# Indirect DMAs in place of a one-hot product for the int4 weight's permutation, and another step order ahead of the first FFN

## The chip, the cores and the metric

One core of a Trainium2 chip runs the whole program in one launch. The metric is the time on the device in microseconds (us), the median of several runs. TensorE is called PE below, VectorE DVE, ScalarE ACT, GpSimd POOL, SyncE SP.

## What is computed

Two gated layers over 8 batches of 128 tokens with 512 features. Each layer is cross attention (32 query heads, 8 key/value heads, head size 128, keys and values from a context of 128 tokens), then a feed-forward part:

```python
x = x + tanh(g_xattn[0]) * xattn(layernorm(x), ctx, mask, ...)      # layer 0
x = x + tanh(g_ffn[0]) * mx_ffn(layernorm(x), w_gate, w_up, w_down) # fp6 x fp4 block quantised, 1376 inner
x = x + tanh(g_xattn[1]) * xattn(layernorm(x), ctx, mask, ...)      # layer 1
x = x + tanh(g_ffn[1]) * int4_linear(layernorm(x))                  # this change
# int4_linear: y = x[:, perm] @ w.T + bias, w (512 x 512) from int4 pairs and a scale per 128 inputs
```

The columns of x are permuted by `perm`. The kernel permutes the weight instead: row `i` of the transposed weight has to stand at row `perm[i]`.

## The kernel before

**Units and steps.** A unit is one key/value group (with its 4 query heads) of one batch: 64 units a layer, 128 in all. The program runs in steps, one unit a step, software-pipelined: in step n PE makes K, V and Q of unit n (`three_products`, L1210), the scores of unit n-1 (L1274), the transposes of the probabilities of unit n-2 (L1202) and, at the end of the step, their product with V (`values`, L1301), and the output projection of unit n-3 (L1210, from oT). In between stand the transposes of the scaled K (L1291) and Q (L1202, from qn). Every fp32 product is three products of split operands (`_hi` and `_lo`, 4 k-tiles each).

**Kinds of steps.** 0 to 7 are FIRST. 8 to 47 are QUANT: beside attention they quantise one piece each of the first FFN's weight. 48 to 87 are ZONE, written out one by one: 48 to 55 still quantise pieces but run in the plain order, 56 (`FFN0`) to 74 hold the FFN's tiles (norm at 56, gate at 57, down at 58, and so on, a new tile every second step), and from 75 (`INT4_0`) on the int4 weight is made. 88 to 119 are PLAIN, the rest LAST, where the last linear layer runs with the permuted weight `wp_hi`, `wp_lo`. All engines run the same list of steps, each with its own code in the order written in its `step`.

**Order within a step.** In a QUANT step PE does the scores ahead of the probabilities' transposes, ACT does the exponentials of the unit before at the step's start (`exp_after`) and kT, DVE does qn ahead of the row maximum, and POOL subtracts the split weight (`split_lower`, L494) behind the rounding of the piece (`round_piece`, L532 to L537). In the other steps the probabilities come first, kT is DVE's (L1070), and POOL's splits stand at the step's start, ahead of `unit_rstd` (L519, L523). `unit_rstd` waits for ACT's sums of squares (L694); K's and Q's scaling, and so PE's transposes L1291 and L1202, wait for it.

**Weights.** SP loads each group's weight (`load_group`: wq, wk, wv once `kv_ps` and `q_ps` say that the slot is free, wo once `y_ps` does). ACT rounds 10 pieces of 512 columns to `w_hi` (L661), POOL subtracts (L494). Pieces 0 to 3 are Q's, 4 and 5 K's and V's, 6 to 9 wo's. `SPLIT_ZONE` says at which ZONE step each is done.

**The int4 weight before.** `int4_weights` (DVE, 8 parts in steps 75 to 82): two one-hot matrices from an iota of POOL's and `perm` (L955), nibbles (L961, L962), scaling (L969), and the split into `w4_hi` and `w4_lo` (L975, L979). In each of the steps 83 to 86 PE multiplies them with the one-hots in 8 matmuls of 512 columns (L1407). ACT copies `wp_hi` (L762), DVE `wp_lo` (L1104).

Of the kernel before, what the change touches and what calls it, by code (L numbers as in the profile page):

```python
# [14 lines left out]
P = 128  # L15
# [82 lines left out]
SPLIT_ZONE = {1: ((B, 0), (B, 1)), 2: ((B, 2), (B, 3)), 3: ((B, 4), (B, 5)), 4: ((B, 6), (B, 7)), 5: ((B, 8), (B, 9)),  # L98
# [34 lines left out]
INT4_PARTS = 8  # L133
# [19 lines left out]
def flamingo_kernel(nc, x, ctxT, mask, g_xattn, g_ffn, norms, wq, wk, wv, wo, ffn_w,  # L153
                    packedT, scalesT, perm, bias, out):
    top = ExitStack()
    with top:
# [3 lines left out]
        def sem(name):  # L160
# [22 lines left out]
        w4_hi = sb("w4_hi", [P, 2, 2, D], FP32R, under)  # L183
        w4_lo = sb("w4_lo", [P, 2, 2, D], FP32R, under)
# [58 lines left out]
        perm_f = sb("perm_f", [P, 2, 2])  # L243
# [41 lines left out]
        loaded_w4, loaded_bias, iota_done, nibbles, w4_scaled, w4_done, wp_ps, wp_hid, wp_lod, biased = (sem(n) for n in (  # L285
            "loaded_w4", "loaded_bias", "iota_done", "nibbles", "w4_scaled", "w4_done", "wp_ps", "wp_hid", "wp_lod", "biased"))
# [60 lines left out]
        def gathered(n, kind):  # L347


            at = n - INT4_0 - INT4_PARTS  # L350
            return (at,) if kind == ZONE and 0 <= at < KT else ()
# [5 lines left out]
        def qn_first(kind, t):  # L357

            return kind in (FIRST, QUANT) or t.down is not None or t.next is not None

        def exp_after(kind):

            return kind == QUANT
# [19 lines left out]
        def _(sp):  # L383
# [75 lines left out]
            sp.dma_start(perm_sb[:, :, :], perm.rearrange("(t p c) -> p t c", t=2, c=2)).then_inc(loaded_w4, 16)  # L459
            load_group(E, 0, None, step_of(C, BATCHES - 1) + 1)  # L460
            load_group(E + 1, 1)
            sp.wait_ge(wp_ps, KT)
            sp.dma_start(bias_sb[:, :], bias.partition_broadcast(P)).then_inc(loaded_bias, 16)
# [14 lines left out]
        def _(pool):  # L478
# [74 lines left out]
            def step(n, b, kind, j, q=None):  # L553
# [13 lines left out]
                if kind in (ZONE, PLAIN):  # L567
                    split_lower(split_pieces(n, b, kind, j))
# [943 lines left out]
```

## Time and profile before

| | us |
|---|---|
| median of 3 runs | 1347.76 |
| lowest and highest of them | 1346.44, 3458.26 |
| the profiled execution, whole | 1346.49 |
| its span in the profile | 1344.6 |
| PE busy | 1336.9 (99%) |
| DVE, ACT, POOL busy | 960.4, 837.0, 635.2 |

1.9 us of the profiled execution lie outside its span. The granted TensorE clock is full in all 40 slices. The sum of the prediction is made against 1346.49, which is 1.3 below the median and within 0.1 of the lowest run. PE's busy time comes from modelled ends of pipelined matmuls, so where PE stands is better read from the distance between starts of the same row in successive steps.

### The profile page before, as it was taken

To read this page: it belongs to the slowest core of one execution; us is meant where nothing else is said; L and a number is where in the kernel's file an instruction comes from. 1 tells how busy PE (TensorE), PEld (TensorE's weight loads), DVE (VectorE), ACT (ScalarE), POOL (GpSimd) and SP (SyncE) were. 2 spreads that over 40 slices of the span, in tenths; PEclk is the share of its full clock that TensorE was granted. 3 is DMA by queue.
4 is the path that set the end of the run, shared out by engine and by line. 5 is a ranking of instruction groups with operands and counts; after the bars stand their busy time and mean duration, and the time that the engine had idled before them with its cause. 6 is when DMAs were issued, how large, how long until landed. Compare 5 with 4: busy or idle time off the path is not lost.

```text
span 1344.6 us, 25713 instructions
## 1 busy us (share of the span) xinstructions
PE 1336.9 (99%) x7841; PEld 1135.6 (84%) x7841; DVE 960.4 (71%) x1984; ACT 837.0 (62%) x3299; POOL 635.2 (47%) x682
## 2 busy tenths in 40 slices
PE   9999999999999999999999999999999999999999
PEld 7888888888888888777777788888888888888887
DVE  6878787887878798788888857766555555555656
ACT  6767676676767675556656556655666656565542
POOL 3456556564646575356767424432434333332232
PEclk9999999999999999999999999999999999999999
DMA  8011212102121210010100022001010100100001
GB/s 291 1 60 50 67 50 65 52 22 64 49 66 49 67 50 21 1 48 32 49 32 1 1 79 79 32 1 56 32 47 31 45 33 0 47 31 1 2 8 56
DMA packets 32957, 59.49 MB, mean 44 GB/s; under 512 B 2928, under 2 KB 24304, under 8 KB 28784
## 3 DMA queue, kind: packets, MB, share of 16 engines
q1 hardware_dynamic: 32592, 58.01, 13.0%
q8 instruction: 39, 0.64, 0.2%
q10 hardware_dynamic: 288, 0.52, 0.1%
q14 instruction: 38, 0.31, 0.1%
HBM read 56.43 MB, written 2.10 MB: 44 GB/s over the span
## 4 chain that ended last, share of the span: by engine, by line
PE 96%; DVE 1%; POOL 1%; issue 1%; DMA 0%; ACT 0%; SPq 0%; POOLq 0%; DVEq 0%; ACTq 0%
PE bank L1210 66%; PE bank L1202 9%; PE bank L1274 8%; PE bank L1301 7%; PE bank L1236 3%; PE bank L1395 1%; PE bank L1291 1%; PE bank L1407 1%; DMA w_raw<-in_wv 0%; DVE w_lo L823 0%; PE bank L1382 0%; POOL probs L560 0%; POOL rstd L523 0%; DVE probs L1046 0%; POOL f_s L513 0%
## 5 line engine op out<-in xcount | busy, mean ns | idle before, releaser
L494 POOL TENSOR_TENSOR w_lo<-w_raw,w_hi (+1 forms) x150 | 210.7, 1420 | 174.9 <-ACT w_hi L661 174.9
L694 ACT ACTIVATE squares<-bank 128x128 bf16<-128x128 f32 x512 | 134.4, 278 | 196.3 <-PE bank L1210 196.3
L1046 DVE SCALAR_TENSOR_TENSOR probs<-bank,mask_sb 128x512 f32<-128x512 f32 x127 | 87.6, 690 | 205.6 <-PE bank L1274 190.8
L642 ACT ACTIVATE probs<-probs,negmax 128x128 f32<-128x128 f32 x512 | 198.4, 392 | 7.0 <-DVE negmax L929 4.5
L519 POOL TENSOR_TENSOR meansq<-sumsq,scalars 128x5 f32<-128x5 f32 x128 | 28.1, 219 | 359.1 <-ACT squares L694 359.1
L523 POOL TENSOR_TENSOR rstd<-meansq,scalars 128x5 f32<-128x5 f32 x128 | 153.1, 1196 | 10.8 <-POOL meansq L519 1.1
L1210 PE MATMUL bank<-w_hi,oT_hi 128*128 (+1 forms) x512 | 151.1, 417 | 0.0
L1210 PE MATMUL bank<-w_hi,xT_hi 128*128 (+1 forms) x512 | 141.1, 396 | 0.0
L1210 PE MATMUL bank<-w_lo,oT_hi 128*128 (+1 forms) x512 | 138.1, 391 | 0.0
L1210 PE MATMUL bank<-w_hi,oT_lo 128*128 (+1 forms) x512 | 137.9, 391 | 0.0
L1210 PE MATMUL bank<-w_lo,xT_hi 128*128 (+1 forms) x512 | 137.6, 390 | 0.1
L1210 PE MATMUL bank<-w_hi,xT_lo 128*128 (+1 forms) x512 | 137.3, 390 | 0.0
L1274 PE MATMUL bank<-kT,qT 128*128 128x128 f32 x1024 | 135.0, 275 | 0.0
L1274 PEld LDWEIGHTS bank<-kT,qT 128*128 128x128 f32 x1024 | 127.5, 191 | 3.3
L1210 PEld LDWEIGHTS bank<-w_lo,oT_hi 128*128 128x128 f32 x512 | 96.1, 188 | 22.4
L1210 PEld LDWEIGHTS bank<-w_lo,xT_hi 128*128 128x128 f32 x512 | 96.1, 188 | 22.0 <-DVE w_lo L823 0.8
L1210 PEld LDWEIGHTS bank<-w_hi,oT_lo 128*128 128x128 f32 x512 | 96.1, 188 | 21.2
L1210 PEld LDWEIGHTS bank<-w_hi,xT_lo 128*128 128x128 f32 x512 | 96.1, 188 | 19.9
L1003 DVE TENSOR_TENSOR oT_lo<-bank,oT_hi 128x512 fp32r<-128x512 f32 x125 | 84.1, 673 | 34.7 <-ACT oT_hi L670 34.5
L650 ACT ACTIVATE kn<-bank,rstd 128x128 f32<-128x128 f32 x128 | 47.1, 368 | 97.7 <-POOL rstd L523 97.7
L694 ACT ACTIVATION_READ_ACCUMULATOR squares<-bank 128x1 f32 x512 | 106.8, 209 | 0.0
L1210 PEld LDWEIGHTS bank<-w_hi,xT_hi 128*128 128x128 f32 x512 | 88.1, 189 | 12.9 <-ACT w_hi L617 1.0
(143 smaller groups left out, 3058.7 us busy)
## 6 DMA issues: line engine op xcount, KB each, us to landing
w_raw<-in_wq SPq DMA_DIRECT2D x16, 1024.0 KB, 4.9
w_raw<-in_wo SPq DMA_DIRECT2D x16, 1024.0 KB, 4.8
fw_raw<-in_ffn_w SPq DMA_DIRECT2D x36, 192.0 KB, 2.3
w_raw<-in_wk SPq DMA_DIRECT2D x16, 256.0 KB, 5.3
w_raw<-in_wv SPq DMA_DIRECT2D x16, 256.0 KB, 5.4
x_sb<-in_x SPq DMA_DIRECT2D x7, 256.0 KB, 9.6
ctx_raw<-in_ctxT SPq DMA_DIRECT2D x7, 256.0 KB, 9.1
fw_raw<-in_ffn_w SPq DMA_DIRECT2D x7, 256.0 KB, 2.7
```

Of the source, the lines that this page charges most:

```text
L494: last = nc.gpsimd.tensor_tensor(lo, raw, hi.bitcast(FP32), ALU.subtract)
L523: nc.gpsimd.tensor_tensor(rstd[:, :], meansq[:, :], minus_half[:, :], ALU.pow).then_inc(rs_done, 1)
L642: last = nc.scalar.activation(probs[:, h * P:(h + 1) * P], probs[:, h * P:(h + 1) * P], ACT.Exp, bias=negmax[:, h:h + 1], accum_out=rowsum ...
L650: nc.scalar.activation(kn[:, :], kv_bank(n, kind)[:, 0:P], ACT.Copy, scale=rstd[:, REP:REP + 1]).then_inc(kn_done, 1)
L694: last = nc.scalar.activation(squares[:, h // 2, (b + 1) % 4, h % 2, :], q_bank(n, kind)[:, h * P:(h + 1) * P], ACT.Square, scale=SCALE, a ...
L1003: nc.vector.tensor_tensor(oT_lo[:, :], psPO[:, :], oT_hi[:, :].bitcast(FP32), ALU.subtract).then_inc(o_lod, 1)
L1046: nc.vector.scalar_tensor_tensor(heads(probs[:, :]), heads(psSQ[:, :]), SCALE, mask_sb[:, :].unsqueeze(1).to_broadcast([P, REP, P]), ALU.m ...
L1202: last = nc.tensor.transpose(dst[:, k * P:(k + 1) * P], src[:, k * P:(k + 1) * P], m)
L1210: last = nc.tensor.matmul(dst, left(a, k), right(b, k), start=(n == 0), stop=(n == len(terms) - 1))
L1236: last = nc.tensor.matmul(ps[:, 0:width], f_xqT[:, k, :], wT[:, col:col + width], start=(k == 0), stop=(k == KT - 1))
L1274: last = nc.tensor.matmul(psSQ[:, h * P:(h + 1) * P], qT[:, h * P:(h + 1) * P], kT[:, :], start=True, stop=True)
L1301: last = nc.tensor.matmul(psPO[:, :], v[:, slot, :], p[:, :], start=(k == 0), stop=(k == 2))
```

## The change

1. **The permutation.** One-hots, iota, `w4_hi`/`w4_lo` and PE's products go. `int4_weights` has 4 parts (nibbles, scaling, twice), in steps 75 to 78. POOL writes the scaled rows to a DRAM tensor `w4_rows`, row `perm[i]`, by two indirect DMAs at the end of its step 77 and two at the end of 79. SP reads it back into `w4_turned` (1 MB) behind the wo load of group E+2, when all four are done. In steps 83 to 86, as before, ACT makes `wp_hi` and DVE `wp_lo`, now from `w4_turned`, and `wp_lo` by subtracting `wp_hi`. The bias load stands ahead of these loads.
2. **The order.** `calm` is QUANT and ZONE up to step 55: steps 48 to 55 get the order of the QUANT steps on PE, ACT, DVE and POOL. Group B's pieces move one step earlier or closer together: three in 49, three in 50, two in 51, two in 52.
3. **The first FFN norm.** In step 56 POOL's `ln_rstd_of` for tile 0 stands ahead of `unit_rstd`.

```diff
-SPLIT_ZONE = {1: ((B, 0), (B, 1)), 2: ((B, 2), (B, 3)), 3: ((B, 4), (B, 5)), 4: ((B, 6), (B, 7)), 5: ((B, 8), (B, 9)),
+SPLIT_ZONE = {1: tuple((B, k) for k in range(3)), 2: tuple((B, k) for k in range(3, 6)), 3: ((B, 6), (B, 7)), 4: ((B, 8), (B, 9)),
...
-INT4_PARTS = 8
+INT4_PARTS = 4
+GATHER0 = INT4_0 + 8
...
+        def calm(n, kind):
+
+            return kind == QUANT or (kind == ZONE and n < FFN0)
...
+            sp.wait_ge(w4_scattered, 4 * 16)
+            sp.dma_start(w4_turned[:, :, :], w4_rows.rearrange("(k p) o -> p k o", p=P)).then_inc(w4_back, 16)
...
-                if kind in (ZONE, PLAIN):
+                if kind in (ZONE, PLAIN) and not calm(n, kind):
                     split_lower(split_pieces(n, b, kind, j))
+                if t.norm == 0:
+                    ln_rstd_of(NORM["ffn", t.norm])
...
-                if kind == ZONE and n == INT4_0:
-                    pool.wait_ge(d_ps, BATCHES)
-                    nc.gpsimd.iota(iota_i, pattern=[[1, D]], base=0, channel_multiplier=0).then_inc(iota_done, 1)
+                if kind == ZONE and n in (INT4_0 + 2, INT4_0 + 4):
+
+                    t4 = (n - INT4_0) // 2 - 1
+                    pool.wait_ge(w4_scaled, t4 + 1)
+                    for c in range(2):
+                        nc.gpsimd.indirect_dma_start(
+                            w4_rows, bass.IndirectOffsetOnAxis(perm_sb[:, t4, c:c + 1].bitcast(U32), 0),
+                            w4[:, t4, c, :], None).then_inc(w4_scattered, 16)
...
                 for k in gathered(n, kind):
 
-                    act.wait_ge(wp_ps, k + 1)
-                    nc.scalar.activation(wp_hi[:, k, :], psA[:, :], ACT.Copy).then_inc(wp_hid, 1)
+                    act.wait_ge(w4_back, 16)
+                    nc.scalar.activation(wp_hi[:, k, :], w4_turned[:, k, :], ACT.Copy).then_inc(wp_hid, 1)
...
-                    dve.wait_ge(wp_ps, k + 1)
-                    nc.vector.tensor_copy(wp_lo[:, k, :], psB[:, :]).then_inc(wp_lod, 1)
+                    dve.wait_ge(wp_hid, k + 1)
+                    nc.vector.tensor_tensor(wp_lo[:, k, :], w4_turned[:, k, :], wp_hi[:, k, :].bitcast(FP32),
+                                            ALU.subtract).then_inc(wp_lod, 1)
```

DVE in one of the steps 49 to 54, before (line numbers of the old kernel), from the masking of the scores on:

```order
L1046 SCALAR_TENSOR_TENSOR probs<-bank,mask_sb 128x512
L929 TENSOR_REDUCE negmax<-probs 128x4
L942 TENSOR_TENSOR qn<-bank,rstd 128x512
L934 TENSOR_TENSOR pT_lo<-bank,pT_hi 128x512
L1070 TENSOR_SCALAR kT<-bank,scalars 128x128
L1082 SCALAR_TENSOR_TENSOR x_sb<-bank,scalars,x_sb 128x512
L925 RECIPROCAL rinv<-rowsum 128x4
L877 STREAM_TRANSPOSE fw_turned<-fw_out 128x384
```

The same place in the changed program (its own line numbers):

```order
L1029 SCALAR_TENSOR_TENSOR probs<-bank,mask_sb 128x512
L936 TENSOR_TENSOR pT_lo<-bank,pT_hi 128x512
L944 TENSOR_TENSOR qn<-bank,rstd 128x512
L931 TENSOR_REDUCE negmax<-probs 128x4
L1065 SCALAR_TENSOR_TENSOR x_sb<-bank,scalars,x_sb 128x512
L879 STREAM_TRANSPOSE fw_turned<-fw_out 128x384
```

The row maximum went behind pT_lo and qn, kT went to ACT, and the reciprocal to a later place of the next step.

POOL in steps 56 and 57 before: unit 56's rstd, then the FFN norm's, its normalised tile f_s, and the next step's scaling of the quantised tile and of the probabilities.

```order
L560 TENSOR_TENSOR probs<-probs,rinv 128x512
L519 TENSOR_TENSOR meansq<-sumsq,scalars 128x5
L523 TENSOR_TENSOR rstd<-meansq,scalars 128x5
L504 TENSOR_SCALAR ln_var<-ln_mv 128x1
L507 TENSOR_TENSOR ln_rstd<-ln_var,scalars 128x1
L513 TENSOR_SCALAR f_s<-x_sb,ln_mv,ln_rstd 128x512
L549 TENSOR_TENSOR f_xq<-f_xq,blk_pow 128x512
L560 TENSOR_TENSOR probs<-probs,rinv 128x512
```

The same in the changed program:

```order
L555 TENSOR_TENSOR probs<-probs,rinv 128x512
L499 TENSOR_SCALAR ln_var<-ln_mv 128x1
L502 TENSOR_TENSOR ln_rstd<-ln_var,scalars 128x1
L514 TENSOR_TENSOR meansq<-sumsq,scalars 128x5
L518 TENSOR_TENSOR rstd<-meansq,scalars 128x5
L508 TENSOR_SCALAR f_s<-x_sb,ln_mv,ln_rstd 128x512
```

The two small instructions of the norm stand ahead of the unit's two.

POOL in steps 77 to 80 of the changed program; before, the same rows stood there without the two DMA rows.

```order
L489 TENSOR_TENSOR w_lo<-w_raw,w_hi 128x512 x2
L514 TENSOR_TENSOR meansq<-sumsq,scalars 128x5
L518 TENSOR_TENSOR rstd<-meansq,scalars 128x5
L597 DMA w_rows<-w,perm_sb 512x512 x2
L489 TENSOR_TENSOR w_lo<-w_raw,w_hi 128x512 x2
L514 TENSOR_TENSOR meansq<-sumsq,scalars 128x5
L518 TENSOR_TENSOR rstd<-meansq,scalars 128x5
L489 TENSOR_TENSOR w_lo<-w_raw,w_hi 128x512 x2
L514 TENSOR_TENSOR meansq<-sumsq,scalars 128x5
L518 TENSOR_TENSOR rstd<-meansq,scalars 128x5
L597 DMA w_rows<-w,perm_sb 512x512 x2
L489 TENSOR_TENSOR w_lo<-w_raw,w_hi 128x512 x2
```

Each pair of DMAs stands between a step's rstd and the next step's two splits. On PE the change takes out `L1407 MATMUL bank<-w_hi,onehot 128x512 x4` and its partner with `w_lo`, four times, and nothing else but the order of scores and probabilities in steps 48 to 55.

## Rows read from the trace of the kernel before

**Rows 1.** Page, parts 1 and 4: busy time; chain that ended last.

```profile
PE 1336.9 (99%) x7841; PEld 1135.6 (84%) x7841; DVE 960.4 (71%) x1984; ACT 837.0 (62%) x3299; POOL 635.2 (47%) x682
...
PE 96%; DVE 1%; POOL 1%; issue 1%; DMA 0%; ACT 0%; SPq 0%; POOLq 0%; DVEq 0%; ACTq 0%
```

**Rows 2.** Chain in order of time (start, us, what): steps 84, 87.

```profile
879.19 4.19 PE bank L1210 x24
...
913.25 4.19 PE bank L1210 x24
```

**Rows 3.** The chain in order of time: steps 46, 47 and 55.

```profile
443.76 4.19 PE bank L1210 x24
453.29 4.19 PE bank L1210 x24
...
531.22 4.20 PE bank L1210 x24
```

**Rows 4.** Line L855 (ns min/median/max), 430 to 530 us alone.

```profile
L855 DVE TENSOR_SCALAR amax<-amax x9: 157/1057/1064, 437.7 to 524.6; 128x12 f32<-128x12 f32 x8, 128x16 f32<-128x16 f32 x1
```

**Rows 5.** POOL in order of time, step 45; in brackets the idle time before.

```profile
444.09 1.30 POOL L494 TENSOR_TENSOR w_lo<-w_raw,w_hi  x1
449.20 0.19 POOL L519 TENSOR_TENSOR meansq<-sumsq,scalars 128x5 f32<-128x5 f32 x1 [3.82 <-ACT squares L694]
```

**Rows 6.** POOL and DVE in order of time, step 50.

```profile
484.04 3.00 POOL L494 TENSOR_TENSOR w_lo<-w_raw,w_hi 128x512 fp32r<-128x512 f32 x2 [0.76 <-ACT w_hi L661]
...
486.00 1.06 DVE L855 TENSOR_SCALAR amax<-amax 128x12 f32<-128x12 f32 x1
```

**Rows 7.** DVE, POOL in order of time, step 56; then PE's wait.

```profile
543.71 0.18 DVE L805 BATCH_NORM_AGGREGATE ln_mv<-ln_stats 128x2 f32<-128x6 f32 x1
...
546.19 0.20 POOL L519 TENSOR_TENSOR meansq<-sumsq,scalars 128x5 f32<-128x5 f32 x1 [4.33 <-ACT squares L694]
...
548.66 2.08 POOL L513 TENSOR_SCALAR f_s<-x_sb,ln_mv,ln_rstd 128x512 f32<-128x512 f32 x1
...
550.78 0.69 DVE L887 TENSOR_REDUCE amax<-f_s 128x16 f32<-128x512 f32 x1 [0.96 <-POOL f_s L513]
...
PEld bank L1202 <- POOL probs L560: 0.8, 1, 0.8
```

**Rows 8.** POOL in order of time, steps 79 and 80.

```profile
835.45 1.17 POOL L523 TENSOR_TENSOR rstd<-meansq,scalars 128x5 f32<-128x5 f32 x1
840.48 3.33 POOL L494 TENSOR_TENSOR w_lo<-w_raw,w_hi 128x512 fp32r<-128x512 f32 x2 [3.87 <-ACT w_hi L661]
844.70 0.19 POOL L519 TENSOR_TENSOR meansq<-sumsq,scalars 128x5 f32<-128x5 f32 x1 [0.89 <-ACT squares L694]
```

**Rows 9.** SP's issues: scale_sb (ns), its landings, x_sb (page, 6).

```profile
L457 SPq DMA_DIRECT2D scale_sb<-in_scalesT x4: 596/602/1001, 772.6 to 774.9; - x4
...
DMA to landing us min/median/max: 3.5/3.9/4.5
...
x_sb<-in_x SPq DMA_DIRECT2D x7, 256.0 KB, 9.6
```

**Rows 10.** SP, ACT, DVE in order of time, steps 82 to 84.

```profile
866.62 0.33 SPq L394 DMA_DIRECT2D w_raw<-in_wo  x1
...
w_raw<-in_wo SPq DMA_DIRECT2D x1, 1024.0 KB, 4.9
...
876.76 0.60 ACT L751 ACTIVATE qT<-bank 128x512 f32<-128x512 f32 x1
...
880.95 1.79 DVE L1017 TENSOR_TENSOR probs<-probs,rinv 128x512 f32<-128x512 f32 x1
```

**Rows 11.** SP and ACT in order of time: wo of group B, step 51.

```profile
491.12 0.33 SPq L394 DMA_DIRECT2D w_raw<-in_wo  x1
...
493.06 1.14 ACT L661 ACTIVATE w_hi<-w_raw 128x512 fp32r<-128x512 f32 x2
...
496.74 0.28 ACT L694 ACTIVATE squares<-bank 128x128 bf16<-128x128 f32 x1 [2.11 <-PE bank L1210]
```

More of the change, by code:

```diff
@@ L355, in quant_piece, with qn_first @@
             return q * QSTEPS + b
[L357 to L363, printed above, removed]
+        def calm(n, kind):
+            return kind == QUANT or (kind == ZONE and n < FFN0)
+        def qn_first(n, kind, t):
+            return kind == FIRST or calm(n, kind) or t.down is not None or t.next is not None
         def kv_bank(n, kind):
@@ L576, in step @@
                     scale_six(1, t.down)
-                if t.norm is not None:
+                if t.norm is not None and t.norm:
                     ln_rstd_of(NORM["ffn", t.norm])
@@ L683, in step @@
                 split_upper(late_pieces(n, kind))
-                if kind == QUANT:
+                if calm(n, kind):
                     split_upper(split_pieces(n, b, kind, j))
@@ L988, in step @@
                 if has(n, 2):
-                    if kind != QUANT:
+                    if not calm(n, kind):
                         row_inverse(n)
@@ L1012, in step @@
                     piece_maximum(q, b)
-                if kind == QUANT:
+                if has(n, 2) and calm(n, kind):
                     row_inverse(n)
@@ L1048, in step @@
                         mask_sb[:, :].unsqueeze(1).to_broadcast([P, REP, P]), ALU.mult, ALU.add).then_inc(masked, 1)
-                if has(n, 1) and not qn_first(kind, t):
+                if has(n, 1) and not qn_first(n, kind, t):
                     maximum(n)
-                if has(n, 2) and (t.gate is not None or kind == QUANT):
+                if has(n, 2) and (t.gate is not None or calm(n, kind)):
                     probs_lower(n)
@@ L1054, in step @@
                     scaled_q(n, kind, t)
-                if has(n, 2) and qn_first(kind, t) and kind != QUANT:
+                if has(n, 2) and qn_first(n, kind, t) and not calm(n, kind):
                     probs_lower(n)
-                if has(n, 1) and qn_first(kind, t):
+                if has(n, 1) and qn_first(n, kind, t):
                     maximum(n)
-                if has(n, 2) and t.gate is None and not qn_first(kind, t):
+                if has(n, 2) and t.gate is None and not qn_first(n, kind, t):
                     probs_lower(n)
@@ L1064, in step @@
                     xT_lower(2 * BATCHES + t.last)
-                if has(n, 0) and not t.active and kind != QUANT:
+                if has(n, 0) and not t.active and not calm(n, kind):
                     dve.wait_ge(kt_ps, n + 1)
@@ L1355, in step @@
                     probabilities()
-                if has(n, 1) and kind != QUANT:
+                if has(n, 1) and not calm(n, kind):
                     scores()
```

81 lines of the change are left out of this document (23 added, 58 removed).

## The prediction

> **What bounds the kernel now.** I read the page first: PE is busy 1336.9 of 1344.6 us and makes up 96% of the chain that ended last [rows 1]. So only what PE executes, or what PE waits for, moves the time; DVE, ACT and POOL matter where they are late for PE. The second view is the chain in order of time. Every step has one long row, the 24 matmuls of K's last and Q's first products up to Q's end, and the distance between two such rows is the length of a step. Undisturbed it is 9.53 (453.29 - 443.76, [rows 3]). Two stretches are longer and the change touches both, and a third place is a single wait.
>
> **1. PE's one-hot products go.** From step 84's row to step 87's, with the one-hot products of steps 84 to 86 in between, the chain takes 913.25 - 879.19 = 34.06, 11.35 a step [rows 2]. The extra 1.82 is eight matmuls of 512 columns at 0.23, PE's own work and no wait. There are four such steps: 4 x 1.82 = **7.3 us** go. Nothing of PE's comes in their place, since the weight now comes back by a DMA.
>
> What takes the products' place has to be hidden, and I go through it by engine.
>
> DVE loses more than it gets in steps 75 to 82; with the old parts these steps ran at 9.53, so I price it at 0.
>
> POOL gets two indirect DMAs behind rstd in step 77 and two in 79. Queued behind them are the next step's two splits, then the mean square and rstd that K's and Q's scaling wait for. In step 79 to 80 POOL's rstd ends at 836.62, the splits start at 840.48 after 3.87 idle, and before the mean square it is idle 0.89 again [rows 8]. So a pair of DMAs has 3.87 + 0.89 = 4.8 us before the mean square comes late. No row shows POOL issuing a DMA. The bound from below is an issue of SP, 0.6 us each [rows 9]: a pair 1.2, no loss. The bound from above is that POOL stands still until a transfer has landed, as long as the small broadcasts took, 4.5 us at most [rows 9]: a pair 9.0, 4.2 too long, twice, 8.4 us lost. I take the lower end's side, up to 2.4 us for one, because building a transfer is all that the program asks of POOL and it waits for no landing there; price 0, with 8.4 as the far end.
>
> A sentence of the Trainium skill speaks against this step: "DMA: Bandwidth & Descriptors", section SWDGE vs HWDGE vs iDMA, says that a DMA issued from GpSimd has its descriptors written by GpSimd's cores into SBUF, and that VectorE in its two-port modes locks them out. No run here shows that yet. By its fixed cost (the same page, Anatomy of one DMA, about 2.0 us each, mostly the receipt) a pair would be 4.0, an estimate, and still within 4.8 if all of it were POOL's.
>
> SP reads 1 MB back behind the wo load of step 82. That wo load is issued at 866.62, and such a load lands after 4.9 [rows 10]. The readback is issued 0.4 later and moves as much; one after the other they end by 866.62 + 2 x 4.9 = 876.4. ACT comes to the first copy when qT is done, 877.36 [rows 10]. So it is hidden with 1 us to spare; behind it ACT has oT_hi and the next splits. The copies themselves are no new work (ACT and DVE made the same tiles from PSUM). But DVE's scaling of the probabilities (L1017) took 1.79 beside POOL's split in step 84 [rows 10]; without PE's 1.84 the same chain has less room, and it can come a few tenths late. I take 0 for it, with 0.3 in each of four steps, 1.2, as the bound.
>
> **2. Steps 48 to 55 in the QUANT order.** From step 47's row to step 55's are 531.22 - 453.29 = 77.93 for eight steps, 1.69 more than 8 x 9.53 = 76.24 [rows 3]. The cause is on DVE. In these steps POOL's splits lie over DVE's scaling of the piece: L855, 12 numbers a partition, begins at 486.00 and ends at 487.06, when POOL's splits of 484.04 to 487.04 end [rows 6]; of the nine between 430 and 530 us, seven of them in steps 48 to 54 and five of those in the steps with splits, the fastest takes 0.16 and the median 1.06 [rows 4]. DVE is then late with the masking, qn and pT_lo, and PE loses 0.2 a step. In QUANT steps the split starts behind the rounding (444.09) and is over when DVE comes to L855, and POOL still idles 3.82 [rows 5]. So the new order gives the **1.7 us** back.
>
> The Trainium skill has this as a rule ("SBUF — State Buffer", section Who interferes with whom: the port pair shared by VectorE and GpSimd is an exclusive lock for a whole instruction); the trace agrees, 1.06 against 0.16.
>
> It isn't free. Steps 49 and 50 now have three splits. From 444.09 that is 3 x 1.3 = 3.9, to 448.0, before the mean square at 449.20 [rows 5], so POOL isn't late; but the third piece lies over L855, which can then wait up to 0.9. Between nothing and 0.6 of it reaches PE, in two steps; before, 0.9 of blocked L855 cost PE 1.69 / 8 = 0.2 a step, and I take 0.15 each. In step 51 ACT now wants wo's pieces 6 and 7. Their load is issued at 491.12 in step 50 [rows 11] and lands 4.9 later, at 496.0; two pieces (1.14, [rows 11]) end at 497.2, and the squares, at 496.74 before [rows 11], come 0.4 late. That costs between 0 and 0.4; I take 0.1. Together **+0.4**, at most 1.6.
>
> **3. The first FFN norm.** POOL idles 4.33 for the squares, makes the mean square at 546.19 and rstd (1.17 long, [rows 8]) to 547.65, then ln_rstd, and f_s from 548.66 [rows 7]. DVE waits 0.96 for f_s, and at the end of this line (f_xq, then the probabilities on POOL) PE waits 0.8 [rows 7]. With ln_rstd made in POOL's idle 4.33, f_s can start at 547.7, 1.0 earlier, DVE is free for it by its own wait of 0.96, and PE's wait is gone: **-0.8**. For ln_rstd to fit, the moments must be there 1.0 ahead of the squares. They were ready at 543.89, 2.3 ahead [rows 7]; in the new order of step 56 ACT's exponentials and with them DVE's reciprocal come later, by about 1. If it doesn't fit, unit_rstd is late by what is lacking, 1.0 at most: between -0.8 and +1.0. It fits with 0.3; I take -0.8.
>
> **The sum.** -7.3 - 1.7 + 0.4 - 0.8 = -9.4. From 1346.5, the profiled execution's own time, that is 1337.1. The median of the three runs stood 1.3 above it; I say **1337.3**.
>
> **The rivals.**
>
> A. *The order of steps 48 to 55 gains nothing*: three splits in a row and the late wo pieces take as much as the order gives, or the switch of order at 56 costs what the one at 48 did. For it: L855 and the third piece do meet. Against it: only two steps have three, and the order is proven for 40 steps at 9.53. Time: 1337.1 + 1.7 + 1.2 = 1340.0.
>
> B. *The readback is late*: scattered rows or a wait of SP put it behind 877.4. Each us that it lacks over one or so goes straight to PE through ACT's oT_hi. At twice the wo load's 4.9 it costs 4: 1341.
>
> C. *POOL's DMAs are long, moderately*: above 2.4 us each the mean square comes late. At 4.5 each, 8.4: 1345.5. The skill's rule of the locked port ("DMA: Bandwidth & Descriptors") would make this case likelier.
>
> D. *Slower than before, by the same place*: POOL held at L597 in steps 77 and 79 for as long as the slowest kind of load took, 9.6 us [rows 9]. A pair is 19.2, 14.4 too long, twice: 28.8 lost, 1366. It decides from (9.4 + 2 x 4.8)/4 = 4.75 us per DMA on. For it: no row shows POOL's price. Against it: the 9.6 is mostly queueing behind other loads at the start.
>
> **How the numbers follow.** Forecast 0.63 (1335.8 to 1338.9: nothing lost on the far side, or 0.3 more in the gather steps and the medians' 1.3), A 0.13, B 0.07, C 0.11, D 0.06. The range reaches from the forecast's low end over A and B to 1341.0; C and D, 0.17, are left out. About 2%, 27 us, is what a measurement of this kernel is taken to tell from no change. None of the cases but the far end of D (1374 would take 11 us per DMA) reaches it: faster 0.01, same 0.97, slower 0.02.
>
> **What the new profile should show.** The rows of K and Q 9.53 apart from step 76 to 88, with no one-hot row; the same from 47 to 55, with at most 0.3 more at 49 to 51; L855 at 0.16 but for one or two; step 57's probabilities without POOL in front. Wrong would be: a mean square in steps 78 and 80 that waits for POOL's own DMAs and not for ACT's squares, kn and qn behind it, and PE idle ahead of L1275's transposes; or ACT idle at `wp_hi` in step 83 until the DMA, with PE waiting for oT_lo. The prediction is wrong in its main term if the steps 83 to 86 stay above 9.6.

## The result and the profile after

| | before | after |
|---|---|---|
| median of 6 runs, us | 1346.76 | 1339.99 |
| lowest to highest of after | | 1338.46 to 1341.13 |
| profiled execution, span | 1344.6 | 1338.5 |
| PE busy | 1336.9 | 1328.1 |

The ratio is 0.9948, 95% interval 0.9938 to 0.9958: 6.8 us less in the medians, 6.1 in the two spans. One of the six runs of before took 3458.26; the ratio goes by the fast runs alone. The forecast was 1337.3 with a range to 1341.0, so the time lies in the range, 2.7 above the forecast. It lies outside the forecast's own band of 1335.8 to 1338.9, in the part of the range that was kept for rivals A and B.

The chain of the kernel after, in order of time (start, length, what). L1194 is what L1210 was. The first rows are the steps whose one-hot products went, and answer to [rows 2]:

```profile
878.36 4.20 PE bank L1194 x24
...
906.94 4.20 PE bank L1194 x24
```

The two are three steps apart, 28.58 or 9.53 a step, and between them is no one-hot row: 1.82 less in each of four steps. The same chain at steps 47 to 55, the answer to [rows 3]:

```profile
454.99 4.19 PE bank L1194 x24
...
474.06 4.19 PE bank L1194 x24
...
493.43 4.18 PE bank L1194 x24
...
531.55 4.19 PE bank L1194 x24
```

531.55 - 454.99 = 76.56 for eight steps, where it had been 77.93. What is left over 76.24, 0.3 us, lies between 474.06 and 493.43 (19.37 for two steps). DVE's L855 is now L857, again from 430 to 530 us alone (ns minimum/median/maximum), to be read beside [rows 4]:

```profile
L857 DVE TENSOR_SCALAR amax<-amax x9: 157/165/1061, 439.4 to 525.2; 128x12 f32<-128x12 f32 x8, 128x16 f32<-128x16 f32 x1
```

The median fell from 1057 to 165 ns. Two of the nine still take 1.05 or more: the one at 487.23 lies ahead of the row at 493.43 and its lost 0.3, the one at 496.74 costs nothing. Step 56, POOL in order of time, the answer to [rows 7]:

```profile
545.25 0.19 POOL L499 TENSOR_SCALAR ln_var<-ln_mv 128x1 f32<-128x1 f32 x1 [0.56 <-DVE ln_mv L807]
545.52 0.56 POOL L502 TENSOR_TENSOR ln_rstd<-ln_var,scalars 128x1 f32<-128x1 f32 x1
546.53 0.20 POOL L514 TENSOR_TENSOR meansq<-sumsq,scalars 128x5 f32<-128x5 f32 x1 [0.46 <-ACT squares L696]
546.81 1.17 POOL L518 TENSOR_TENSOR rstd<-meansq,scalars 128x5 f32<-128x5 f32 x1
547.98 2.08 POOL L508 TENSOR_SCALAR f_s<-x_sb,ln_mv,ln_rstd 128x512 f32<-128x512 f32 x1
```

ln_rstd fits ahead of the squares with 0.46 us to spare, and f_s follows rstd at once.

Steps 79 and 80 are where the new kernel is worse. POOL in order of time, to be read beside [rows 8]:

```profile
817.16 1.22 POOL L597 DMA_INDIRECT w_rows<-w,perm_sb  x1 [0.19 <-issue]
818.69 0.96 POOL L597 DMA_INDIRECT w_rows<-w,perm_sb  x1 [0.30 <-issue]
820.84 3.00 POOL L489 TENSOR_TENSOR w_lo<-w_raw,w_hi 128x512 fp32r<-128x512 f32 x2 [1.19 <-ACT w_hi L663]
...
836.20 1.04 POOL L597 DMA_INDIRECT w_rows<-w,perm_sb  x1 [0.18 <-issue]
842.51 0.96 POOL L597 DMA_INDIRECT w_rows<-w,perm_sb  x1 [5.26 <-issue]
843.50 2.55 POOL L489 TENSOR_TENSOR w_lo<-w_raw,w_hi 128x512 fp32r<-128x512 f32 x2
845.99 0.21 POOL L514 TENSOR_TENSOR meansq<-sumsq,scalars 128x5 f32<-128x5 f32 x1
846.28 1.19 POOL L518 TENSOR_TENSOR rstd<-meansq,scalars 128x5 f32<-128x5 f32 x1
```

The first pair costs POOL 2.7 us, and the splits behind it still wait for ACT. In the second pair 5.26 us of "issue" stand ahead of the second DMA, an idle time that no semaphore ended, and the mean square waits for POOL's own queue. Undisturbed it would stand at 834.58 + 9.53 = 844.11; it is 1.9 late. The chain in order of time runs through this place:

```profile
837.25 5.26 issue
...
846.28 1.20 POOL rstd L518
...
847.50 0.38 ACT kn L652
...
847.92 0.33 PE bank L1275
```

The DMAs there: SP's by the issues view from 833 to 845 us (KB, us from issue to landing), then the landings of L597's four:

```profile
w_raw<-in_wq SPq DMA_DIRECT2D x1, 1024.0 KB, 5.4
w_raw<-in_wk SPq DMA_DIRECT2D x1, 256.0 KB, 5.8
w_raw<-in_wv SPq DMA_DIRECT2D x1, 256.0 KB, 6.5
```

```profile
DMA to landing us min/median/max: 2.7/2.8/5.8
```

The third indirect DMA, issued at 836.20 beside SP's 1.5 MB, is the one of 5.8: it lands at 842.0, and the fourth starts 0.5 later.

The steps can be compared by the start of K's transposes (L1275, L1291 before). This table, worked out from them for all profiles, gives in us the time from the span's start to step 8, the excess over 9.53 a step in three stretches, the length of step 56, and the time from step 8 to step 127:

| profile | to 8 | 47-55 | 56 | 76-83 | 83-87 | 8 to 127 |
|---|---|---|---|---|---|---|
| before | 89.6 | 1.68 | 12.34 | 0.0 | 7.29 | 1220.3 |
| before, second profile | 89.5 | 1.68 | 12.33 | 0.0 | 7.29 | 1220.3 |
| before + DRAM tensor | 90.5 | 1.71 | 12.36 | 0.0 | 7.29 | 1220.4 |
| before + scatters | 89.5 | 1.71 | 12.36 | 1.15 | 7.29 | 1221.5 |
| after | 91.3 | 0.32 | 11.47 | 1.57 | 0.0 | 1212.3 |
| after, second profile | 91.0 | 1.90 | 11.47 | 2.01 | 0.0 | 1214.4 |
| scratch 576 | 89.9 | 0.34 | 11.47 | 0.53 | 0.0 | 1211.4 |
| scratch 256 | 91.1 | 0.33 | 11.47 | 1.20 | 0.0 | 1212.0 |
| old order | 91.5 | 1.69 | 11.47 | 1.79 | 0.0 | 1213.9 |
| two splits | 91.0 | 0.14 | 11.47 | 0.88 | 0.0 | 1211.5 |
| rstd back | 90.8 | 0.35 | 12.34 | 0.89 | 0.0 | 1212.6 |
| four in step 80 | 91.2 | 0.33 | 11.48 | 4.03 | 0.0 | 1214.9 |
| one a step | 90.1 | 0.15 | 11.47 | 0.0 | 0.0 | 1210.6 |
| one a step, wo later | 89.8 | 0.14 | 11.47 | 0.0 | 0.0 | 1210.6 |

From before to after: -7.3, -1.4, -0.9 and +1.6, together -8.0, and +1.7 ahead of step 8, in which nothing of PE's work was changed. The experiments take these apart.

### The profile page after: what moved, and what is told of

Read it like the earlier page. It is cut to its first block, busy times and chain, and to the rows that moved or that the text cites. A ratio compares the mean times of both kernels' runs of the same rounds, so it can differ in the third digit from the quotient of the medians.

```text
span 1338.5 us, 25627 instructions
## 1 busy us (share of the span) xinstructions
PE 1328.1 (99%) x7809; PEld 1129.1 (84%) x7809; DVE 951.5 (71%) x1967; ACT 840.4 (63%) x3307; POOL 635.5 (47%) x685
## 3 DMA queue, kind: packets, MB, share of 16 engines
q0 software_dynamic: 320, 1.05, 0.2%
## 4 chain that ended last, share of the span: by engine, by line
PE 95%; DVE 1%; POOL 1%; issue 1%; DMA 0%; ACT 0%; SPq 0%; POOLq 0%; DVEq 0%; ACTq 0%
PE bank L1194 66%; PE bank L1186 9%; PE bank L1258 8%; PE bank L1285 7%; PE bank L1220 3%; PE bank L1379 1%; PE bank L1275 1%; DMA w_raw<-in_wv 0%; POOL w_lo L489 0%; DVE w_lo L825 0%; POOL rstd L518 0%; PE bank L1366 0%; DVE probs L1029 0%; POOL w_rows L597 0%; POOL f_iq L544 0%
## 5 line engine op out<-in xcount | busy, mean ns | idle before, releaser
L1194 PE MATMUL bank<-w_hi,oT_hi 128*128 (+1 forms) x512 | 151.1, 417 | 0.0
L1194 PE MATMUL bank<-w_hi,xT_hi 128*128 (+1 forms) x512 | 141.3, 397 | 0.2 <-ACT w_hi L619 0.2
L1194 PE MATMUL bank<-w_lo,oT_hi 128*128 (+1 forms) x512 | 138.2, 392 | 0.0
L1194 PE MATMUL bank<-w_hi,oT_lo 128*128 (+1 forms) x512 | 137.9, 391 | 0.0
L1194 PE MATMUL bank<-w_lo,xT_hi 128*128 (+1 forms) x512 | 137.5, 390 | 0.1
L1194 PE MATMUL bank<-w_hi,xT_lo 128*128 (+1 forms) x512 | 137.3, 390 | 0.0
L1194 PEld LDWEIGHTS bank<-w_lo,oT_hi 128*128 128x128 f32 x512 | 96.1, 188 | 22.4
L1194 PEld LDWEIGHTS bank<-w_lo,xT_hi 128*128 128x128 f32 x512 | 96.1, 188 | 21.9 <-DVE w_lo L825 0.7
L1194 PEld LDWEIGHTS bank<-w_hi,oT_lo 128*128 128x128 f32 x512 | 96.1, 188 | 21.2
L1194 PEld LDWEIGHTS bank<-w_hi,xT_lo 128*128 128x128 f32 x512 | 96.1, 188 | 19.9
L1194 PEld LDWEIGHTS bank<-w_hi,xT_hi 128*128 128x128 f32 x512 | 88.0, 189 | 13.3 <-ACT w_hi L619 1.4
```

Source lines behind the costliest of these rows:

```text
L1194: last = nc.tensor.matmul(dst, left(a, k), right(b, k), start=(n == 0), stop=(n == len(terms) - 1))
```

## The experiments

**The fourth indirect DMA: scratch of 576 bytes.** The scratch is the space that the program sets aside for POOL's software DMAs (`dynamic_dma_scratch_size`). The kernel before has 256 bytes of it; the change also raised it to 512, a line that the excerpt of the diff leaves out. My theory was that POOL waited because its descriptor scratch was full; the rival, that SP's loads held it up.

```diff
-    nc = bacc.Bacc("TRN2", target_bir_lowering=False, num_devices=1, dynamic_dma_scratch_size=512)
+    nc = bacc.Bacc("TRN2", target_bir_lowering=False, num_devices=1, dynamic_dma_scratch_size=576)
```

> The changed kernel with one number altered: the scratch space for POOL's software descriptors is 576 bytes a partition and not 512. In the changed kernel the fourth indirect DMA shows 5.26 us of issue ahead of it (836.20 to 842.51), and steps 79 and 80 are 1.14 and 0.45 us over 9.53. Theory (ring): the fourth DMA found the scratch full behind three others and waited until the third had landed, which took 5.8 us beside SP's loads of wq, wk and wv. A slightly larger scratch holds a fourth if one takes 144 bytes or less of it: the 5.26 shrinks to under 0.5, the steps come back to about 9.6 each, the whole is about 1.5 us shorter than the changed kernel, near 1338.5. If one takes more than 144, nothing changes, and the theory is neither shown nor refuted. Rival (contention): SP's three loads, issued 833.4 to 834.9, hold POOL up whatever the scratch: 5.26 and 1.6 us stay, and the smaller scratch of the next run shows the same 5.26 in the second pair and nothing new in the first.

Measured: 1338.12, ratio to before 0.9936 (0.9920 to 0.9953). POOL:

```profile
834.83 1.04 POOL L597 DMA_INDIRECT w_rows<-w,perm_sb  x1 [0.18 <-issue]
840.08 0.96 POOL L597 DMA_INDIRECT w_rows<-w,perm_sb  x1 [4.21 <-issue]
```

The wait is there, so 576 bytes don't take a fourth. It is 1.05 shorter than in the kernel after because the third landed in 4.7 and not in 5.8. Of the 2.4 us between the two profiles 1.0 is this landing and 1.4 the start. Both vary with a scratch of 512 too (the landing from 5.1 to 6.2 beside a second pair in step 79), so I don't put them down to the larger scratch; one profile can't rule that out. A much larger scratch wasn't tried.

**Scratch of 256 bytes.** The same line with 256.

> The changed kernel with the scratch space for POOL's software descriptors halved, 256 bytes and not 512. Ring theory: one or two DMAs fill it, so the second or third DMA waits for the landing of the one before it: the first pair, which shows 0.19 and 0.30 us of issue at 817.2 and 818.7, now shows about 1.7 to 2 us ahead of its second DMA (median landing 2.8 us less the instruction's own 1.0), and the second pair again about 5 us. Step 77 or 78 then grows by up to about 1 us (the splits there had 1.19 us of waiting for ACT to give), and steps 79 and 80 stay at 10.7 and 10.0. Contention rival: the first pair stays at 0.2 and 0.3 and the time is that of the changed kernel.

```profile
816.91 1.22 POOL L597 DMA_INDIRECT w_rows<-w,perm_sb  x1 [0.19 <-issue]
820.38 0.97 POOL L597 DMA_INDIRECT w_rows<-w,perm_sb  x1 [2.25 <-issue]
...
835.95 1.05 POOL L597 DMA_INDIRECT w_rows<-w,perm_sb  x1 [0.18 <-issue]
841.91 0.96 POOL L597 DMA_INDIRECT w_rows<-w,perm_sb  x1 [4.91 <-issue]
```

Time 1339.49. Now the second DMA waits too, where no load of SP's is near: the scratch decides which DMA waits. The pair in step 77 was expected to cost up to 1 us and cost nothing: the splits behind it then run back to back, 2.54 for two and not 3.00, and the mean square behind them still waits 0.89 for the squares. The time, of a single run, is no longer than with 512, so no gain of the raised scratch shows here.

**The old order in steps 48 to 55.**

```diff
-            return kind == QUANT or (kind == ZONE and n < FFN0)
+            return kind == QUANT
-                if calm(n, kind) or (kind == ZONE and n == FFN0):
+                if calm(n, kind) or (kind == ZONE and n == ZONE0):
-SPLIT_ZONE = {1: tuple((B, k) for k in range(3)), 2: tuple((B, k) for k in range(3, 6)), 3: ((B, 6), (B, 7)), 4: ((B, 8), (B, 9)),
+SPLIT_ZONE = {1: ((B, 0), (B, 1)), 2: ((B, 2), (B, 3)), 3: ((B, 4), (B, 5)), 4: ((B, 6), (B, 7)), 5: ((B, 8), (B, 9)),
```

> The changed kernel with the second part of the change undone: steps 47 to 55 go back to the order of the kernel before (splits ahead of the rounding, the old table of weight pieces, ACT's exp where it was); the scatter and the early first FFN norm stay. My accounting of the two profiles gives the second part 1.40 us (steps 48 to 54 from a mean of 9.77 to 9.53, less 0.30 at step 50). Expected: 1.4 us slower than the changed kernel, near 1341.4, with steps 47 to 54 at 9.69 to 9.99 again. Rival: the gain was the two profiles' own difference or is handed back at step 56: then the time is within 0.4 us of the changed kernel.

Measured: 1341.87, ratio 0.9955 (0.9939 to 0.9972). The chain, step 47 and step 55, and L857 in the same stretch as above:

```profile
455.15 4.19 PE bank L1194 x24
...
533.09 4.20 PE bank L1194 x24
```

```profile
L857 DVE TENSOR_SCALAR amax<-amax x9: 156/1056/1062, 439.6 to 526.4; 128x12 f32<-128x12 f32 x8, 128x16 f32<-128x16 f32 x1
```

Eight steps in 77.94 again, 1.38 more than with the new order, and step 56 stays at the 11.47 of the kernel after. The second part is worth 1.4, and nothing of it is handed back.

But the excess isn't spread evenly over the steps, as the prediction had it. In the kernel before, the chain, and DVE in the first of these steps:

```profile
473.07 4.18 PE bank L1210 x24
...
521.71 4.18 PE bank L1210 x24
```

```profile
465.03 0.18 DVE L925 RECIPROCAL rinv<-rowsum 128x4 f32<-128x4 f32 x1 [2.65 <-ACT probs L642]
467.09 0.17 DVE L855 TENSOR_SCALAR amax<-amax 128x16 f32<-128x16 f32 x1
```

From 453.29 [rows 3] to 473.07 are two steps in 19.78, 0.7 too many, and the only L855 in that place took 0.17: nothing blocked it. The chain goes there through ACT's exponentials, the reciprocal, which waited 2.65 for them, and DVE's work up to qn. The five steps from 473.07 to 521.71 lose 0.20 each, and these are the five whose L855 took 1.06. The step behind them, with an L855 of 0.17, is 9.51. The old order in the changed kernel shows the same (19.79 for the first two steps). So the blocked L855 stands for 1.0 of the 1.7 us; 0.7 was the price of the first step of the stretch, and which part of the new order takes that away no run tells. The changed kernel switches its order in step 56 instead, and there the rows stay 9.53 apart.

**Two splits a step and no more.**

```diff
-SPLIT_ZONE = {1: tuple((B, k) for k in range(3)), 2: tuple((B, k) for k in range(3, 6)), 3: ((B, 6), (B, 7)), 4: ((B, 8), (B, 9)),
+SPLIT_ZONE = {0: ((B, 0), (B, 1)), 1: ((B, 2), (B, 3)), 2: ((B, 4), (B, 5)), 3: ((B, 6), (B, 7)), 4: ((B, 8), (B, 9)),
```

> The changed kernel with the ten w_lo pieces of group B dealt two to each of steps 48 to 52, and not three, three, two, two to steps 49 to 52: no step has three POOL splits any more. Theory: the 0.30 us that step 50 lost (9.83 against 9.53) is the third split beside DVE's L857, which took 1.05 us where it takes 0.6, and pushed mask, qn and PE by 0.25; with two splits all steps from 47 to 54 are 9.53 and the time falls by 0.3 us, near 1339.7. Rival: the 0.30 came from ACT's late w_hi pieces and the landing of wo, or is noise of one profile: step 50 or another keeps a 0.3 us excess. A second rival: step 48 has no room for two pieces, because wq, wk and wv of the group have only just landed, and a new wait of 0.3 us or more stands there.

Measured: 1339.59, ratio 0.9943 (0.9926 to 0.9959). L857 and the chain from step 47 to 50:

```profile
L857 DVE TENSOR_SCALAR amax<-amax x9: 155/158/165, 439.1 to 524.7; 128x12 f32<-128x12 f32 x8, 128x16 f32<-128x16 f32 x1
```

```profile
473.72 4.19 PE bank L1194 x24
483.37 4.18 PE bank L1194 x24
492.90 4.19 PE bank L1194 x24
```

No L857 is blocked any more, and the 0.30 of step 50 is gone: the third split was its cause. But 0.12 stand in the step before it (9.65), so the gain is 0.18 and not 0.3; in the chain they are the four transposes of qn, 0.56 where they take 0.44 elsewhere, and why is open.

**One indirect DMA a step, with two splits.**

```diff
-                if kind == ZONE and n in (INT4_0 + 2, INT4_0 + 4):
+                if kind == ZONE and INT4_0 + 2 <= n < INT4_0 + 6:
-                    t4 = (n - INT4_0) // 2 - 1
+                    t4, c4 = divmod(n - INT4_0 - 2, 2)
-                    for c in range(2):
+                    for c in (c4,):
```

> The changed kernel with two edits: the ten w_lo pieces of group B dealt two to each of steps 48 to 52, as in the run above with two splits, and the four indirect DMAs issued one in each of steps 77, 78, 79 and 80 where two stood in 77 and two in 79. Theory (the fourth DMA waits for the landing of the third; its 4.6 to 5.5 us of issue in five profiles was the third's landing of 4.7 to 5.9 us less 0.5 each time, and with half the scratch the second DMA waited 2.25 us behind the first's 2.8): with a step of 9.53 us between any two, each finds the one before landed, so none shows more than 0.3 us of issue, the third lands late beside SP's loads and nobody waits for it, and steps 79 and 80 come to 9.53. Against the changed kernel: less 1.6 there, less 0.2 at step 50, so a time near 1338.0 and a ratio near 0.993. Rival (SP's loads hold POOL up by themselves): the third or the fourth DMA, in step 79 or 80, still shows 4 to 5 us and 1 us or more stays.

Measured: 1337.53, ratio 0.9933 (0.9920 to 0.9947). POOL in step 79, then the landings of the four:

```profile
834.87 1.04 POOL L597 DMA_INDIRECT w_rows<-w,perm_sb  x1 [0.20 <-issue]
838.51 3.00 POOL L489 TENSOR_TENSOR w_lo<-w_raw,w_hi 128x512 fp32r<-128x512 f32 x2 [2.61 <-ACT w_hi L663]
```

```profile
DMA to landing us min/median/max: 2.8/2.9/6.4
```

The third DMA is issued beside the same loads of SP's and lands even later, after 6.4; POOL spends 1.04 on it and goes on. Every step from 76 to 87 is 9.53. So the loads don't hold POOL; they hold the transfer, and POOL waits for it only where a further DMA is issued before it has landed and the scratch has no room.

**The kernel before, a second profile**, unaltered.

> The kernel before, unaltered, for a second profile. In its first profile the first K was transposed 19.88 us after the span's start, in the five of the changed kernel and its variants at 21.49, 20.09, 21.26, 21.66 and 21.23; ACT waited there for wv's landing (0.60, against 0.88 to 2.54 us). Theory: how fast the first loads land varies from run to run, whatever the kernel, since nothing ahead of step 70 of the DMAs was changed: this second profile lies anywhere from 19.9 to 21.7, and one above 20.5 shows it. Rival: the change itself makes the start 1 to 1.6 us longer, for instance by where its tensors lie in DRAM: then this profile is again at 19.9, within 0.2.

Time 1346.34, first K at 19.35. My theory wanted anything from 19.9 to 21.7; it lies below all of them. The rival wanted 19.9 within 0.2, and it misses that too, on the early side.

**The kernel after, a second profile**, unaltered.

> The changed kernel, unaltered, on the same chip as the others of this call. Expected: about 1339.9 (1338.5 to 1341), the fourth indirect DMA again with its issue time 0.5 us under the third's landing, steps 79 and 80 together 0.5 to 1.8 us over 19.06, and the sum of the first K's time and that excess explaining the spread between its runs. Start-up theory: the first K between 19.9 and 21.7 us. Rival: 21.3 to 21.7 as in most profiles of the changed kernel.

Measured: 1340.19, ratio 0.9945 (0.9930 to 0.9960). The fourth DMA as expected, and one thing that wasn't. ACT in step 51, first in the kernel after, then in this profile, both answering to [rows 11], and this profile's landing of wo:

```profile
496.68 1.15 ACT L663 ACTIVATE w_hi<-w_raw 128x512 fp32r<-128x512 f32 x2 [0.67 <-DMA w_raw<-in_wo]
```

```profile
498.42 1.15 ACT L663 ACTIVATE w_hi<-w_raw 128x512 fp32r<-128x512 f32 x2 [2.71 <-DMA w_raw<-in_wo]
```

```profile
q8 instruction: 1, 0.02, 0.6%
...
w_raw<-in_wo SPq DMA_DIRECT2D x1, 1024.0 KB, 6.8
```

wo took 6.8 us where it takes 4.6 to 4.9 in the other thirteen profiles. The first line, of the same view (488 to 500 us), is one transfer of 16 KB of a queue that the profile calls instruction. It began 0.1 us after wo's issue; in the thirteen others none falls in this load. There are 196 loads of wo in the fourteen profiles, without the first two of each. The fifteen with such a transfer beside them landed after 5.2 to 6.8, the other 181 after 4.6 to 5.6. Fourteen of the fifteen are one and the same load, near 630 us, and may be late for another reason; the one here is not. So the late landing is put down to this transfer by its company alone; no run moves it. ACT's squares behind it are late, and steps 50 to 51 take 11.14 and 9.80: the 1.90 of the table, 1.6 more than the first profile.

**The first FFN norm behind rstd again.**

```diff
-                if t.norm == 0:
-                    ln_rstd_of(NORM["ffn", t.norm])
-                if t.norm is not None and t.norm:
+                if t.norm is not None:
```

> The changed kernel with its third part undone: POOL computes the first FFN norm's ln_rstd behind the step's rstd again and not ahead of it, as the kernel before. Theory: step 56 goes from 11.47 back to 12.34 us (0.87 more), all else as in the changed kernel. Rival: the 0.87 came from the second part (what stands in steps 47 to 55 no longer pushes work into step 56), and the step stays at 11.5.

Time 1339.84, of a single run and no longer than the kernel after's, since the fourth DMA cost only 0.9 in it. Step 56 is 12.34 again; by the length of the step the third part is worth 0.87.

**The start.** Two kernels add to the kernel before, first, the tensor and one ordinary transfer,

```diff
+    w4_rows = nc.dram_tensor("w4_rows", (D, D), FP32, kind="Internal").ap()
+            sp.wait_ge(consts, 2)
+            sp.dma_start(w4_rows[0:P, 0:P], ident[:, :]).then_inc(rows_written, 16)
```

> The kernel before with one thing added: the 1 MB internal DRAM tensor of the changed kernel, into which SP writes one 64 KB block by an ordinary transfer behind the loading of the permutation (near 780 us), in no one's way; nothing reads it. In two profiles of the kernel before the first K was transposed at 19.88 and 19.35 us, in eight of the changed kernel and its variants between 20.09 and 21.66, mean 21.05: the difference of 1.4 us stands although nothing of the first 70 steps' DMAs was edited. Theory (place): the extra tensor shifts where the weights lie in DRAM and the first loads land later: this profile shows the first K at 20.5 or later. Theory (queue): the indirect DMAs' software queue takes something at the start; then this profile is near 19.6 and the next run near 21. Third: chance, then both lie anywhere.

and then the tensor and four indirect DMAs of the identity's rows:

```diff
+                if kind == ZONE and n in (INT4_0 + 2, INT4_0 + 4):
+                    for c in range(2):
+                        nc.gpsimd.indirect_dma_start(
+                            w4_rows, bass.IndirectOffsetOnAxis(perm_sb[:, t4, c:c + 1].bitcast(mybir.dt.uint32), 0),
+                            ident[:, :], None).then_inc(rows_written, 16)
```

> The kernel before with the internal 1 MB DRAM tensor and four indirect DMAs of POOL, two in step 77 and two in step 79, that scatter 128 rows of 512 bytes each of the identity tile into it by the permutation; nothing reads it, and the one-hot products stay. Start-up: by the queue theory the first K comes at 20.5 to 21.7 us here and at 19.6 in the run above; by the theory of the tensor's place at 20.5 or more in both. POOL: each indirect DMA 1.0 to 1.2 us as in the changed kernel if the cost is in its 128 rows; the second of the second pair again waits for the landing of the first of that pair, which is 64 KB here and not 256: if the landing under SP's loads is shorter than 4.2 us, the wait under 3.7 and steps 79 and 80 stay at 9.53 to 9.6; if the loads ahead of it in the engines make the landing and not its own size, it is 5 us or more again with 1 us or more lost.

Times 1347.82 and 1347.6; the first K at 20.69 and 19.69. Neither theory holds by itself: the kernel with tensor and queue is as early as the kernel before. With the scratch of 256 bytes of the kernel before, the second DMA of each pair waits here too (1.77 and 3.60). A DMA moves 64 KB here and not 256, and beside SP's loads it still lands after 4.1. The wait of 3.60 cost nothing, as expected: steps 79 and 80 stay at 9.53. And a stall came up that I hadn't expected. POOL and DVE in step 77:

```profile
822.10 2.54 POOL L496 TENSOR_TENSOR w_lo<-w_raw,w_hi 128x512 fp32r<-128x512 f32 x2
```

```profile
821.81 3.39 DVE L1027 TENSOR_TENSOR probs<-probs,rinv 128x512 f32<-128x512 f32 x1
```

In the second profile of before the same instruction takes 1.38; there POOL's splits began 0.5 ahead of it. In the changed kernel with a scratch of 256 it takes 0.68 and is over when they begin. Here POOL's late splits begin 0.3 behind it and run back to back, and it ends at 825.20, behind both. In the chain PE waits for it and is 1.15 late for probs. So splits that come late can cost time through DVE, before any rstd is late.

**wo's pieces a step later.** The one-a-step kernel, with wo's pieces where the kernel before had them:

```diff
-SPLIT_ZONE = {0: ((B, 0), (B, 1)), 1: ((B, 2), (B, 3)), 2: ((B, 4), (B, 5)), 3: ((B, 6), (B, 7)), 4: ((B, 8), (B, 9)),
+SPLIT_ZONE = {0: ((B, 0), (B, 1)), 1: ((B, 2), (B, 3)), 2: ((B, 4), (B, 5)), 4: ((B, 6), (B, 7)), 5: ((B, 8), (B, 9)),
```

> The changed kernel with one indirect DMA in each of steps 77 to 80 (as the best version so far), and the pieces of group B's w_lo dealt 0 to 5 to steps 48 to 50 and 6 to 9, which are wo, to steps 52 and 53, where the kernel before had them, and not to 51 and 52. Theory: in the second profile of the changed kernel wo landed 6.8 us after its issue in step 51, where the first took 4.8, ACT stood 2.71 us in front of piece 6, and PE lost 1.6 us; with the piece a step later the landing has 9 us of room and the step stays at 9.53 however slow the load. In the median: as the best version or up to 0.4 us less, 1337.2 to 1337.6 where that had 1337.5, and a narrower spread. Rival: pieces in step 53 meet the first FFN tiles' preparation, and step 53 to 56 lose 0.3 us or more.

Measured: 1337.94 (1336.86 to 1338.14), ratio 0.9934 (0.9920 to 0.9947). In the profile ACT no longer waits for wo; it had waited 0.58 to 2.71 in all eight with pieces 6 and 7 in step 51. Steps 53 to 55 stay at 9.53. The median is the same as that of the kernel it came from within the intervals, which had no late wo in its profile either, so that the pieces' new place brings anything in the time isn't shown. Both medians are 2.0 to 2.7 us under the two of the kernel after (1339.99, 1340.19); the intervals of the ratios overlap, but the excess of steps 76 to 83 is gone in both profiles.

**Four in a row.** All four in step 80, after SP's loads.

```diff
-                if kind == ZONE and n in (INT4_0 + 2, INT4_0 + 4):
+                if kind == ZONE and n == INT4_0 + 5:
-                    for c in range(2):
+                    for t4, c in ((0, 0), (0, 1), (1, 0), (1, 1)):
```

> The changed kernel with all four indirect DMAs in a row at the end of POOL's step 80, behind SP's loads of wq, wk and wv, which have landed by then. Open is how many DMAs the scratch of 512 bytes takes: with it the second of the first pair did not wait and the fourth always did; with 256 bytes and 128 rows of 512 bytes the second waited too. If three fit, only the fourth waits, until the one ahead of it or the first has landed (about 2.2 us of issue or less); if two fit, the third waits already (about 1 to 2.2 us), and the fourth may not. Landings 2.7 to 3 us each without SP's loads beside them. POOL is held 5 to 10 us in all, step 80 and 81 lose 2 us or more, and SP's readback, issued near 868 in the changed kernel, is not late.

Time 1342.53. POOL, then the landings of the four:

```profile
845.68 1.22 POOL L596 DMA_INDIRECT w_rows<-w,perm_sb  x1 [0.19 <-issue]
847.20 0.96 POOL L596 DMA_INDIRECT w_rows<-w,perm_sb  x1 [0.30 <-issue]
848.47 0.96 POOL L596 DMA_INDIRECT w_rows<-w,perm_sb  x1 [0.30 <-issue]
851.72 0.97 POOL L596 DMA_INDIRECT w_rows<-w,perm_sb  x1 [2.29 <-issue]
```

```profile
DMA to landing us min/median/max: 2.7/2.7/3.0
```

Three go out with 0.3 between them, and the fourth waits 2.29 without any load beside it. The first had landed at 845.68 + 3.0 = 848.7 at the latest, and the second, started at 847.20, near 849.9; the third, started at 848.47, lands near 851.2, and the fourth starts at 851.72. So the fourth waited for the landing of the last one ahead of it, not for room of the size of one. Steps 80 and 81 lose 4.0 us together, where I had expected 2 or more.

## Why the prediction was right, and where it was off

The forecast's sum from step 8 on was -9.4; the kernel after shows -8.0, its second profile -5.9, and with the two places mended -9.7.

- *PE's one-hot products*, 7.3: measured 7.3. Steps 83 to 86 are 9.53, so the copies came at no cost on ACT and DVE; the 1.2 held against DVE's part in the bound was 0.
- *The readback*: forecast to land 1 us ahead of ACT. It was issued at 868.00 and landed after 7.4, at 875.4; ACT's first copy stands at 878.25 and waited for nothing. Rival B fell.
- *The indirect DMAs*, priced 0: this step failed. The sizes by themselves were well inside the bound (a DMA is 0.96 to 1.23 of POOL, a pair 2.7, with room 4.8), and the first pair was free. What failed is the reason, that POOL "waits for no landing there": the fourth DMA did wait for a landing. The price was 1.6 and 2.0 in the two profiles of the kernel, 0.5 to 1.8 in its variants with the second pair in step 79, and it follows the third's landing of 4.7 to 6.2. This is rival C's outcome at a fifth of its price, by rival D's mechanism at one of four DMAs. The room was 5.5 and not 4.8, because splits that no longer wait for ACT take 2.55 and not the 3.33 of [rows 8].
- Of the rule of the Trainium skill that VectorE can lock the descriptor writing out ("DMA: Bandwidth & Descriptors", SWDGE vs HWDGE vs iDMA) the runs show nothing clear: of the 44 indirect DMAs in eleven profiles 43 took 0.96 to 1.23, one took 1.40 for a reason not found, and the long waits all end 0.5 after a landing.
- *The order of steps 48 to 55*, -1.7, with +0.3 for the third splits: measured -1.4 in all, by the profile and by undoing it. The sum is right and its reason only in part. The prediction divided 1.69 by eight steps and gave it all to the blocked L855. Five steps with a blocked one lost 0.20 each, 1.0; the other 0.7 stood in step 48, with an L855 of 0.17. That the new order takes this away too follows only from the other argument, that the same order ran at 9.53 in the QUANT steps, and not from L855. The third split's cost was 0.30 in one step and 0 in the other, where I had 0.15 in each. The switch of order in step 56, which rival A feared, costs nothing.
- *wo's late pieces*, 0.1 with 0.4 as the bound: mis-sized. The bound took a landing of 4.9 as fixed. In seven of eight profiles the 0.6 to 0.95 of waiting cost PE nothing, and in one, beside a transfer of the instruction queue, the landing took 6.8 and cost 1.6.
- *The first FFN norm*, -0.8: measured -0.87, also by undoing it alone. The room of 0.3 was 0.46.
- *The start*, not in the sum: to step 8 the four profiles without the change took 89.5 to 90.5, the ten with it 89.8 to 91.5; the means differ by 1.0. ACT waits there for wv, 0.28 to 1.36 in the first four and 0.73 to 2.54 in the others. That this load's landing varies from run to run is plain. Whether the change makes it later on average stays open: neither the tensor nor the software queue, added to the kernel before, showed it.

The 2.7 us between forecast and median are thus about 1.6 for the fourth DMA, sometimes wo, and up to 1 for the start.

That the time lies in the range is in part luck. The range reached to 1341.0 for A and B, and neither came true; what did, POOL waiting for a landing, was C's and D's, which had 0.17 and were left out of it. A's price of 1340.0 lies next to the measured time by chance. It also doesn't fit A's name: with a gain of nothing it would be 1337.1 + 1.7 - 0.4 = 1338.4, and 1340.0 charges the bound of 1.6 on top. And D would need 11.6 us per DMA, not 11, to reach 1374.

## What to carry to other kernels

An engine that issues a DMA can be held by an earlier DMA's landing, and that landing has to be priced at its worst, beside the loads that share the engines. Spread software DMAs out, one a step, rather than in pairs; it took a few lines here and brought 1.6 us. A conversion that reads a fresh load wants room for its slowest landing, not its median. Before an elementwise split is pushed to another place of a step, look at which short instruction of the other vector engine lies there: 0.9 us on twelve numbers a partition cost PE 0.2 us, five times. And don't divide the excess of a stretch by its steps: looked at step by step, 0.7 of 1.7 us here had another cause.

## What the runs showed of the hardware

- With a scratch of 512 bytes three indirect DMAs of 128 rows go out in a row with 0.3 us between them, and the fourth waits until the one ahead of it has landed; with 576 the fourth waits too, and with 256 the second already. The wait ends 0.5 us after that landing: 842.0 and 842.51 in the kernel after, 843.7 and 844.23 in its second profile, 842.0 and 842.53 with rows of 512 bytes.
- An indirect DMA of 128 rows takes POOL 0.96 to 1.23 us (1.40 once), for rows of 2 KB as for rows of 512 bytes. With rows of 2 KB it lands after 2.7 to 3.0, and after 4.7 to 6.4 beside 1.5 MB of ordinary loads. Even 64 KB took 4.1 there and 2.2 to 2.7 without.
- The 1 MB load of wo of group B lands after 4.6 to 4.9 us, but after 6.8 in the one of fourteen profiles where a transfer of 16 KB of the instruction queue began beside it.
- An instruction of DVE can stand through two of POOL's: 3.39 us, where it takes 1.38 when they begin ahead of it and 0.68 with none beside it.
